# Sums of squares of keys and queries: put out by ScalarE's squares, one head at a time, in place of VectorE's sums

## The chip, the cores and the metric

The kernel runs on one core of a Trainium2 chip. The metric is the device time of one execution in microseconds (us), lower is better. The time before is 2769.91 us, the median of three runs (2766.08 to 2769.93).

Engine names as in the profile: PE is TensorE, DVE is VectorE, ACT is ScalarE, POOL is GpSimd, SP is SyncE. PE's weight loads are shown apart, as PEld.

## The reference, cut to what matters

A decoder layer on `x` (4, 256, 512) with a context `ctx` (4, 1601, 512), all fp32: a small attention over features, a cross attention of 32 query heads over 8 key/value heads, and a top-8 router, with a layer norm after each. The cross attention is nearly all of the work:

```
kv = concat([ctx, x])                       # 1857 rows per batch
q = (x @ Wq)  -> 32 heads of 128;  k, v = (kv @ Wk), (kv @ Wv) -> 8 heads of 128
q, k = rms_norm(q), rms_norm(k)             # per row and head: t * rsqrt(mean(t^2) + 1e-6) * w
probs = softmax(q k^T / sqrt(128));  out = (probs v) @ Wo
```

The change is about `mean(t^2)` in the two norms: for each row and head the 128 squares have to be summed.

## The kernel before, in words

One unit `v` is one batch and one key/value head: 4 x 8 = 32 units, some 80 us each. A unit has 15 tiles of key rows (the last has 65 rows) and two halves of 512 queries (2 heads x 256 rows), so 30 score tiles. All engines walk through the same list of steps `s`, one score tile for each step. In a step PE computes the score tile (`S_ps<-QT,KT`), does a piece of other work taken from `fill(s)` (projections of the next unit's keys and values into `K_ps`, of its queries, transposes of keys `KT` and queries `QT`, output products `O`), and multiplies a tile of probabilities that is 20 steps older with V (`OT_ps`). High precision comes from splitting an fp32 operand in a high and a low half and doing three products (lines 1015 to 1017); for some tiles (`FULL`) one plain fp32 product is used (L1045).

ACT in a step, in this order: `exp` of the tile 18 steps back (L1410 the rounded high half `P_hi` where the tile is split, L1411 the full one), the copy and scaling of the new score tile (`copy_scores`, L1397), high halves (`high`), the copies of new keys (`copy_keys`, L1505), `squares`, then the high half of a weight chunk (`split`, L1552). POOL: the low half of the probabilities (`lo`, L932, waits for ACT's L1411), their running sum (`add`, L950), the Newton steps of the rsqrt (`newton`, L959 to L974), low halves of weights (L989, wait for ACT's L1552). DVE: shift of a tile by its maximum (L1743), the running maximum (L1756, L1759, waits for ACT's L1397), the sums of squares, low halves, and what else is small. Each engine's queue is in order.

PE takes a new score tile into one of two banks, so it waits until DVE's running maximum has read the tile two before. It multiplies a split tile of probabilities with V only when POOL's `P_lo` is there.

**The norms.** Keys come in groups of four tiles (the last of three): four groups a unit, each with one `squares` on ACT when its keys are in `nat` (L1522, from SBUF), and the queries in two items a unit (L1526, from the PSUM bank). `sum_squares` on DVE reduces `sq` over each head's 128 columns (L1767, L1770); for queries it also copies the bank to `natq` (L1774) and frees it. So there are 128 + 64 = 192 items. Two steps later ACT's `rsqrt` (L1449, L1451) takes the sums, and POOL's `newton` after it.

Of the kernel before, what the change touches and what calls it, by code (L numbers as in the profile page):

```python
# [21 lines left out]
ACT = mybir.ActivationFunctionType  # L22
AX = mybir.AxisListType
# [22 lines left out]
def layer(nc, x_in, sWq, sbq, sWk, sbk, sWv, sbv, ctx_in, Wq, Wk, Wv, Wo, qw, kw, x1, y_out, Wr, rb, eb, final):  # L46
    B, L, E = ctx_in.shape
    S = x1.shape[1]
    HD = P
    KVH = Wk.shape[1] // HD  # L50
    GR = Wq.shape[1] // HD // KVH
# [38 lines left out]
    GROUPS = [list(range(4 * g, min(4 * g + 4, NJ))) for g in range(-(-NJ // 4))]  # L90
# [3 lines left out]
    def rows_of(j):  # L94
        return P if j < NJ - 1 else TAIL
# [39 lines left out]
    at = (UNITS - 7) * CYCLE - AHEAD  # L135
    ROUTE[at + 4].append(("load weights", 0))
    ROUTE_PE[at + 19].append(("FR",))
    for b in range(B - 1):
        at = (UNITS - 6 + 2 * b) * CYCLE - AHEAD
# [97 lines left out]
    for s in range(WAIT + 4, WAIT + NS):  # L237
        p, j = divmod(s - WAIT, NJ)
# [3 lines left out]
    for t in range(TPB, SELF):  # L242
        at = EVENTS[14 * (t - TPB):14 * (t - TPB) + 14]
# [23 lines left out]
    K_AT = {x: n for n, x in enumerate(K_ITEMS)}  # L267
# [13 lines left out]
    SQ_AT = {x: n for n, (_, x) in enumerate(SQUARED)}  # L281
# [43 lines left out]
    def left(kind, v, at):  # L325
        return NJ * (2 * v - 3) + max(kind[v - 2][at]) + 1 if kind[v - 2][at] else 0
# [8 lines left out]
    with ExitStack() as ctx:  # L335
        def sb(name, shape, dt=F32):
            return ctx.enter_context(nc.sbuf_tensor(name, shape, dt))

        def ps(name):
            return ctx.enter_context(nc.psum_tensor(name, [P, 512], F32))  # L340

        def sem(name):
            return ctx.enter_context(nc.semaphore(name))
# [26 lines left out]
        nat = [sb(f"nat{i}", [P, 4, HD]) for i in range(2)]  # L370
        natq = [sb(f"natq{i}", [P, GR, HD]) for i in range(TPB)]
        sq = sb("sq", [P, 4, HD])
# [65 lines left out]
        ss_k = sb("ss_k", [P, 2, 16])  # L438
        rk = sb("rk", [P, 2, 16])
        ss_q = sb("ss_q", [P, 8])  # L440
# [7 lines left out]
        K_ps = [ps(f"K_ps{i}") for i in range(2)]  # L448
# [121 lines left out]
        s_kr = sem("K_bank_free")  # L570
        s_kc = sem("K_rows_copied")
        s_vh = sem("V_hi_copied")
        s_sq = sem("squares")
        s_ss = sem("sum_of_squares")
        s_ln = sem("log_mean_square")
        s_y0 = sem("rsqrt_estimate")
# [32 lines left out]
        def pair_no(v, q):  # L609
            return 8 * v + q  # L610
# [706 lines left out]
        def _(e):  # L1317
# [175 lines left out]
            def copy_keys(v, q):  # L1493
                js = range(2 * q, min(2 * q + 2, NJ))
                r, k = rows_of(js[-1]), len(js)
                at = 2 * (q % 2)
                src = K_ps[K_AT["P", v, q] % 2][:].rearrange("p (k n) -> p k n", n=2 * HD)
                e.wait_ge(s_kt, 15 * v + js[-1] + 1)
                if q % 2 == 0:
                    g = q // 2  # L1500
                    if g >= 2 or v:

                        e.wait_ge(s_ff, F_AT["KT", v if g >= 2 else v - 1, (g - 2) % 4] + 1)
                        e.wait_ge(s_sq, SQ_AT["K", v if g >= 2 else v - 1, (g - 2) % 4] + 1)
                e.activation(nat[q // 2 % 2][0:r, at:at + k, :], src[0:r, 0:k, 0:HD], ACT.Copy).then_inc(s_kc, 1)  # L1505
                if (v, q) in HALF_PAIR_AT:
                    i = HALF[v].index(js[0])
                    if v >= 2:

                        e.wait_ge(s_pv, left(HALF, v, slice(i, i + k)))  # L1510
                    e.activation(V_hi[v % 2][0:r, i:i + k, :], src[0:r, 0:k, HD:2 * HD], ACT.Copy).then_inc(s_vh, 1)

            def squares(what):
                no = SQ_AT[what]
                if no:

                    e.wait_ge(s_ss, no)
                if what[0] == "K":
                    _, v, g = what
                    k = len(GROUPS[g])  # L1520
                    e.wait_ge(s_kc, pair_no(v, min(2 * g + 1, 7)) + 1)
                    e.activation(sq[:, 0:k, :], nat[g % 2][:, 0:k, :], ACT.Square).then_inc(s_sq, 1)  # L1522
                else:
                    _, v, t = what
                    e.wait_ge(s_qf, 2 * v + t + 1)
                    e.activation(sq[:].rearrange("p h d -> p (h d)"), K_ps[K_AT["Q", v, t] % 2][:], ACT.Square)\  # L1526
                        .then_inc(s_sq, 1)

            def split(chunk):
                n = W_AT[chunk]  # L1530
# [72 lines left out]
        def _(e):  # L1603
# [116 lines left out]
            def opening_self(part, t, i):  # L1720
                if part == "products":
                    self_products(t)
                elif part == "qk sum":
                    self_qk_sum(t, i)
                elif part == "max":
                    self_max(t)
                elif part == "normalise":
                    self_normalise(t)
                elif part == "pv sum":
                    self_pv_sum(t, i)  # L1730
                elif part == "residual":
                    self_residual(t)
                elif part == "layernorm":
                    self_layernorm(t)

            def shift(t):
                p, j = divmod(t, NJ)
                r = rows_of(j)
                if j == 0:
                    e.wait_ge(s_mb, p + 1)  # L1740
                e.wait_ge(s_cp, t + 1)
                d = row[t % RING][0:r, :]
                e.tensor_tensor(d, d, Mb_ps[0:r, :], ALU.add).then_inc(s_d, 1)  # L1743
# [14 lines left out]
                e.wait_ge(s_top, s)  # L1758
                e.scalar_tensor_tensor(a, src, k, a, ALU.mult, ALU.max).then_inc(s_top, 1)  # L1759

            def sum_squares(what):
                no = SQ_AT[what]
                e.wait_ge(s_sq, no + 1)
                if what[0] == "K":
                    _, v, g = what
                    k = len(GROUPS[g])
                    e.reduce_sum(ss_k[:, v % 2, 4 * g:4 * g + k], sq[:, 0:k, :], AX.X).then_inc(s_ss, 1)  # L1767
                else:
                    _, v, t = what
                    e.reduce_sum(ss_q[:, 4 * t:4 * t + 4], sq[:], AX.X).then_inc(s_ss, 1)  # L1770
                    if v:

                        e.wait_ge(s_ff, F_AT["QT", v - 1, 1] + 1)
                    e.tensor_copy(natq[t][:].rearrange("p h d -> p (h d)"), K_ps[K_AT["Q", v, t] % 2][:])\  # L1774
                        .then_inc(s_kr, 1)
# [151 lines left out]
            def block_max(p):  # L1927
                e.wait_ge(s_top, NJ * (p + 1))
                if p:

                    e.wait_ge(s_ff, F_AT["MT", p - 1] + 1)
                e.tensor_reduce(tops[:], top[:].rearrange("p (j a) -> p j a", a=32), AX.X, ALU.max, apply_transpose=True)\
                    .then_inc(s_bm, 1)
# [48 lines left out]
            for s in STEPS:  # L1982
                for part, t, i in SELF_AT[s]:
                    opening_self(part, t, i)
                if 0 <= s - WAIT < NS:
                    shift(s - WAIT)
                if 0 <= s - 1 < NS:
                    raise_max(s - 1)
                if 0 < s < NS and s % NJ == 0:
                    block_max(s // NJ - 1)  # L1990
                for what in squared(s - 1):
                    sum_squares(what)
                for x in fill(s - 1):
                    if x[0] not in ("KV", "Q", "MT") or x == ("MT", HALVES - 1):
                        drain(x)
                for v, q in pairs(s - 1):
                    low_values(v, q)
                for p in divided(s - 2):
                    OT_low(p)
                if s == NS:  # L2000
                    last_blocks()
                if s == NS + WAIT + LAG:
                    last_low()
                if 0 <= s - WAIT - 1 < NS and summed_tile(s - WAIT - 1):
                    sum_tile(s - WAIT - 1)
                for x in fill(s + 1):
                    if x[0] == "AT":
                        sum_blocks(x[1])
                for p in divided(s):
                    divide(p)  # L2010
                for part, t, i in LATER[s]:
                    later(part, t, i)
                for x in fill(s):
                    if x[0] == "MT" and x[1] not in LATE:
                        drain(x)
                for part, b in ROUTE[s]:
                    if part == "stats":
                        x2_stats(b, 2 * b)
                    elif part == "apply":
                        x2_apply(b, 2 * b)  # L2020
                    elif part == "shift":
                        router_shift(b)
                    elif part == "softmax":
                        router_softmax(b)
                    elif part == "top":
                        router_top(b)
                    elif part == "final stats":
                        x2_stats(b, 2 * b + 1)
                    elif part == "final apply":
                        x2_apply(b, 2 * b + 1)  # L2030
# [32 lines left out]
```

## Time and profile before

| | before |
|---|---|
| median of three runs | 2769.91 us |
| the profiled execution's own time | 2767.4 us |
| its span in the profile | 2765.6 us |
| mean granted TensorE clock | 0.993 |
| PE busy | 2694.3 us, 97% of the span |
| POOL busy | 2351.9 us, 85% |
| DVE busy | 2229.7 us, 81% |
| ACT busy | 2092.4 us, 76% |

A busy share is an average over the span; which engine sets the time at a place is read from what an instruction there waits for. In a timeline row the first number is the start in us from the span's start, the second the duration in us; a bracket at its end is the engine's idle time before it and who ended that. Neighbouring instructions of ACT overlap in these rows: the next one starts before the duration of the one before is over, so the distance of two starts is less than a duration. Line numbers (L...) are those of the kernel before.

### The profile page before, as it was taken

Reading aid. Unit: us, or ns where it says so; the run is one execution under the profiler, and the core shown is the slowest. Engines: PE = TensorE matmul, PEld = TensorE weight load, DVE = VectorE, ACT = ScalarE, POOL = GpSimd, SP = SyncE. Lnnn points to the kernel's source line nnn. Section 1 sums busy time; section 2 is a strip of 40 time slices with the busy share of each in tenths; the row PEclk is TensorE's granted clock in tenths of the full one; section 3 lists DMA queues with packets and bytes.
Section 4 is the critical chain, followed back from the end, with each engine's and each line's share of the span. In section 5 each row is a group of like instructions: output and inputs, shape, how many; then the busy total and the mean of one; then the engine's idle time right before and its main releaser. Section 6 shows DMA issues by size and latency. Waiting matters only on the chain.

```text
span 2765.6 us, 47104 instructions
## 1 busy us (share of the span) xinstructions
PE 2694.3 (97%) x14256; PEld 2146.5 (78%) x14256; DVE 2229.7 (81%) x3623; ACT 2092.4 (76%) x4202; POOL 2351.9 (85%) x2300
## 2 busy tenths in 40 slices
PE   7899999999999999999999999999999999999997
PEld 5777777777777788787788888888888887878864
DVE  5488888888888888888888777787777888888887
ACT  2578777787777777777788888788887777777774
POOL 4299999998889888888899888999899888889894
PEclk8999999999999999999999999999999999999999
DMA  6656655665655555555456555445544534444321
GB/s 218 249 198 205 222 194 187 214 209 172 212 176 170 183 180 179 176 188 166 173 173 203 175 184 190 159 171 171 195 158 170 184 130 165 153 164 168 115 66 53
DMA packets 160793, 485.33 MB, mean 175 GB/s; under 512 B 18583, under 2 KB 29337, under 8 KB 160542
## 3 DMA queue, kind: packets, MB, share of 16 engines
q1 hardware_dynamic: 158952, 480.75, 51.3%
q8 instruction: 116, 1.90, 0.3%
q10 hardware_dynamic: 1590, 1.58, 0.2%
q14 instruction: 135, 1.11, 0.1%
HBM read 402.83 MB, written 79.43 MB: 174 GB/s over the span
## 4 chain that ended last, share of the span: by engine, by line
PE 80%; POOL 7%; issue 6%; DVE 5%; ACT 2%; DMA 1%; SPq 0%; POOLq 0%; DVEq 0%; ACTq 0%
PE K_ps L1015 9%; PE K_ps L1017 9%; PE K_ps L1016 9%; PE S_ps L1015 7%; PE OT_ps L1045 7%; PE S_ps L1017 7%; PE S_ps L1016 7%; PE OT_ps L1015 5%; PE OT_ps L1016 5%; PE OT_ps L1017 5%; POOL acc L950 4%; POOL P_lo L932 2%; PE F_ps L1015 2%; PE F_ps L1016 2%; PE F_ps L1017 2%
## 5 line engine op out<-in xcount | busy, mean ns | idle before, releaser
L950 POOL TENSOR_TENSOR acc<-acc,scores 128x512 f32<-128x512 f32 x813 | 1080.5, 1329 | 53.8 <-ACT scores L1411 27.4
L932 POOL TENSOR_TENSOR P_lo<-scores,P_hi 128x512 fp32r<-128x512 f32 x672 | 913.1, 1360 | 186.5 <-ACT scores L1411 184.6
L1759 DVE SCALAR_TENSOR_TENSOR running_max<-S_ps,rk,running_max 128x512 f32<-128x512 f32 (+1 forms) x896 | 667.6, 745 | 274.9 <-ACT scores L1397 272.3
L1397 ACT ACTIVATE scores<-S_ps,rk 128x512 f32<-128x512 f32 (+1 forms) x960 | 650.7, 678 | 74.3 <-PE S_ps L1017 59.4
L1743 DVE TENSOR_TENSOR scores<-scores,Mb_ps 128x512 f32<-128x512 f32 (+1 forms) x960 | 644.5, 671 | 54.1 <-PE Mb_ps L1185 52.8
L1411 ACT ACTIVATE scores<-scores 128x512 f32<-128x512 f32 (+1 forms) x960 | 597.3, 622 | 96.0 <-DVE scores L1743 94.8
L1410 ACT ACTIVATE P_hi<-scores 128x512 fp32r<-128x512 f32 x672 | 423.4, 630 | 270.7 <-DVE scores L1743 193.7
L1015 PE MATMUL S_ps<-QT_hi,KT_hi 128*128 128x512 f32 (+1 forms) x960 | 495.5, 516 | 15.4 <-DVE running_max L1759 14.4
L1015 PE MATMUL K_ps<-Wkv_hi,kvT 128*128 128x256 f32 (+1 forms) x1664 | 470.5, 283 | 8.2 <-DVE kvT L1809 7.8
L1017 PE MATMUL K_ps<-Wkv_hi,kvT 128*128 128x256 f32 (+1 forms) x1664 | 469.6, 282 | 0.0
L1016 PE MATMUL K_ps<-Wkv_lo,kvT 128*128 128x256 f32 (+1 forms) x1664 | 468.7, 282 | 0.0
L1017 PE MATMUL S_ps<-QT_hi,KT_lo 128*128 128x512 f32 (+1 forms) x960 | 379.3, 395 | 0.0
L1016 PE MATMUL S_ps<-QT_lo,KT_hi 128*128 128x512 f32 (+1 forms) x960 | 378.0, 394 | 0.0
L1015 PEld LDWEIGHTS K_ps<-Wkv_hi,kvT 128*128 128x128 f32 (+1 forms) x1664 | 309.1, 186 | 31.4 <-DVE kvT L1809 8.7
L1016 PEld LDWEIGHTS K_ps<-Wkv_lo,kvT 128*128 128x128 f32 (+1 forms) x1664 | 309.2, 186 | 19.7
L1017 PEld LDWEIGHTS K_ps<-Wkv_hi,kvT 128*128 128x128 f32 (+1 forms) x1664 | 309.7, 186 | 0.0
L1015 PE MATMUL OT_ps<-P_hi,V_hi 128*128 128x512 f32 x672 | 286.5, 426 | 13.3 <-POOL P_lo L932 12.8
L1045 PE MATMUL OT_ps<-scores,V_full 128*128 128x512 f32 (+1 forms) x576 | 295.1, 594 | 0.0
L1015 PEld LDWEIGHTS S_ps<-QT_hi,KT_hi 128*128 128x128 f32 (+1 forms) x960 | 177.0, 184 | 139.4 <-issue 59.0
L1016 PE MATMUL OT_ps<-P_lo,V_hi 128*128 128x512 f32 x672 | 265.7, 395 | 0.0
L1017 PE MATMUL OT_ps<-P_hi,V_lo 128*128 128x512 f32 x672 | 265.1, 394 | 0.0
L1016 PEld LDWEIGHTS S_ps<-QT_lo,KT_hi 128*128 128x128 f32 (+1 forms) x960 | 177.9, 185 | 91.5 <-issue 63.0
(256 smaller groups left out, 4619.2 us busy)
## 6 DMA issues: line engine op xcount, KB each, us to landing
kvT<-kvT_scratch SPq DMA_DIRECT2D x403, 512.0 KB, 4.0
Wq_hi<-weight_halves_scratch SPq DMA_DIRECT2D x48, 512.0 KB, 5.8
Wq_lo<-weight_halves_scratch SPq DMA_DIRECT2D x48, 512.0 KB, 6.8
Wo_hi<-weight_halves_scratch SPq DMA_DIRECT2D x48, 512.0 KB, 4.6
Wo_lo<-weight_halves_scratch SPq DMA_DIRECT2D x48, 512.0 KB, 5.8
kvT_scratch<-built SPq DMA_DIRECT2D x45, 512.0 KB, 3.8
rinv_spread<-rinv_scratch SPq DMA_DIRECT2D x63, 256.0 KB, 5.3
Wkv_hi<-weight_halves_scratch SPq DMA_DIRECT2D x24, 512.0 KB, 5.5
```

The source lines that it names most:

```text
L932: e.tensor_tensor(P_lo[n % PB][0:r, :], prob(t)[0:r, :], f(P_hi[n % PB][0:r, :]), ALU.subtract)\
L950: e.tensor_tensor(a[0:r, :], a[0:r, :], prob(t)[0:r, :], ALU.add).then_inc(s_acc, 1)
L1015: e.matmul(out, l_hi, r_hi, start=first, stop=False)
L1016: e.matmul(out, l_hi, r_lo, start=False, stop=False)
L1017: return e.matmul(out, l_lo, r_hi, start=False, stop=last)
L1045: ins = e.matmul(OT_ps[:], V_full[v % 2][0:r, FULL[v].index(j), :], row[t % RING][0:r, :], start=first, stop=last)
L1397: e.activation(row[s % RING][0:r, :], S_ps[s % 2][0:r, :], ACT.Copy, scale=rk[0:r, v % 2, j:j + 1])\
L1410: e.activation(P_hi[n % PB][0:r, :], d, ACT.Exp)
L1411: e.activation(d, d, ACT.Exp).then_inc(s_p, 1)
L1743: e.tensor_tensor(d, d, Mb_ps[0:r, :], ALU.add).then_inc(s_d, 1)
L1759: e.scalar_tensor_tensor(a, src, k, a, ALU.mult, ALU.max).then_inc(s_top, 1)
```

## The change

ACT's square takes `accum_out`, which puts the sum along the free dimension in one column. One such instruction gives one sum for each row, so an item's one instruction over four heads becomes four over 128 columns each (three for the last key group). DVE's sums go; its copy of the queries stays and waits for the last of the four squares. The semaphore of the squares goes, and `s_ss` (the sums) is now counted up by ACT. ACT's wait for DVE's last sum before it overwrites `sq` goes too.

```
@@ copy_keys (ACT)
-                        e.wait_ge(s_sq, SQ_AT["K", v if g >= 2 else v - 1, (g - 2) % 4] + 1)
+                        e.wait_ge(s_ss, SQ_AT["K", v if g >= 2 else v - 1, (g - 2) % 4] + 1)
@@ squares (ACT)
-                if no:
-                    e.wait_ge(s_ss, no)
...
-                    e.activation(sq[:, 0:k, :], nat[g % 2][:, 0:k, :], ACT.Square).then_inc(s_sq, 1)
+                    for i in range(k):
+                        at = 4 * g + i
+                        ins = e.activation(sq[:, i, :], nat[g % 2][:, i, :], ACT.Square, accum_out=ss_k[:, v % 2, at:at + 1])
+                    ins.then_inc(s_ss, 1)
...
-                    e.activation(sq[:].rearrange("p h d -> p (h d)"), K_ps[K_AT["Q", v, t] % 2][:], ACT.Square)\
-                        .then_inc(s_sq, 1)
+                    for h in range(GR):
+                        at = 4 * t + h
+                        ins = e.activation(sq[:, h, :], K_ps[K_AT["Q", v, t] % 2][:, h * HD:(h + 1) * HD], ACT.Square,
+                                           accum_out=ss_q[:, at:at + 1])
+                    ins.then_inc(s_ss, 1)
@@ sum_squares -> copy_queries (DVE)
-                e.wait_ge(s_sq, no + 1)
-                    e.reduce_sum(ss_k[:, v % 2, 4 * g:4 * g + k], sq[:, 0:k, :], AX.X).then_inc(s_ss, 1)
-                    e.reduce_sum(ss_q[:, 4 * t:4 * t + 4], sq[:], AX.X).then_inc(s_ss, 1)
+            def copy_queries(what):
+                if what[0] == "Q":
                     _, v, t = what
+                    e.wait_ge(s_ss, SQ_AT[what] + 1)
```

## Rows read from the trace of the kernel before

**Rows 1.** The page's first part: span, and busy time of each engine.

```profile
span 2765.6 us, 47104 instructions
PE 2694.3 (97%) x14256; PEld 2146.5 (78%) x14256; DVE 2229.7 (81%) x3623; ACT 2092.4 (76%) x4202; POOL 2351.9 (85%) x2300
```

**Rows 2.** Windows: us, then busy us of PE, PEld, DVE, ACT, POOL; clock; DMA.

```profile
100.00:900.00 800.00, 781.76 (x4122) 614.84 (x4121) 658.76 (x1035) 611.68 (x1205) 705.27 (x670) 1.00 0.60 203
900.00:1480.00 580.00, 579.22 (x3104) 466.18 (x3103) 475.54 (x764) 451.11 (x915) 502.90 (x499) 1.00 0.53 179
```

**Rows 3.** Waits of PE from 100 to 2650 us: total us, times, longest.

```profile
PE S_ps L1015 <- DVE running_max L1759: 13.8, 15, 2.3
PE OT_ps L1015 <- POOL P_lo L932: 4.6, 6, 1.8
```

**Rows 4.** ACT's groups by form: count, busy us, mean ns of one, idle before.

```profile
L1522 ACT ACTIVATE sq<-nat 128x512 f32<-128x512 f32 x96 | 60.7, 632 | 4.9 <-ACT nat L1505 0.8
...
L1526 ACT ACTIVATE sq<-K_ps 128x512 f32<-128x512 f32 x64 | 38.2, 598 | 43.2 <-PE K_ps L1017 43.2
...
L1451 ACT ACTIVATE nrm_c<-nrm_c 128x3 f32<-128x3 f32 x32 | 6.5, 204 | 1.0
...
L1368 ACT ACTIVATE self_x<-self_x 128x128 f32<-128x128 f32 x4 | 1.2, 306 | 6.3 <-DVE self_x L1902 6.3
```

**Rows 5.** DVE's groups by form: the sums that go.

```profile
L1767 DVE TENSOR_REDUCE ss_k<-sq 128x4 f32<-128x512 f32 x96 | 64.9, 676 | 49.9 <-ACT sq L1522 49.9
...
L1770 DVE TENSOR_REDUCE ss_q<-sq 128x4 f32<-128x512 f32 x64 | 43.6, 682 | 20.4 <-ACT sq L1526 20.0
...
L1767 DVE TENSOR_REDUCE ss_k<-sq 128x3 f32<-128x384 f32 x32 | 17.6, 552 | 7.1 <-ACT sq L1522 5.6
```

**Rows 6.** Timeline of ACT around the second key group's square, one unit.

```profile
1391.57 1.27 ACT L1437 ACTIVATE natq<-natq,rq 128x128 f32<-128x128 f32 x4
...
1395.98 0.63 ACT L1522 ACTIVATE sq<-nat 128x512 f32<-128x512 f32 x1
1396.52 0.61 ACT L1410 ACTIVATE P_hi<-scores 128x512 fp32r<-128x512 f32 x1
1397.04 0.61 ACT L1411 ACTIVATE scores<-scores 128x512 f32<-128x512 f32 x1
```

**Rows 7.** Timeline of POOL after that square, in three units.

```profile
742.55 2.38 POOL L989 TENSOR_TENSOR Wo_lo<-w_stage,Wo_hi 128x1024 fp32r<-128x1024 f32 x1 [0.81 <-ACT Wo_hi L1552]
...
749.24 1.74 POOL L932 TENSOR_TENSOR P_lo<-scores,P_hi 128x512 fp32r<-128x512 f32 x1
...
1397.73 1.30 POOL L932 TENSOR_TENSOR P_lo<-scores,P_hi 128x512 fp32r<-128x512 f32 x1 [1.24 <-ACT scores L1411]
...
1400.22 1.77 POOL L932 TENSOR_TENSOR P_lo<-scores,P_hi 128x512 fp32r<-128x512 f32 x1
...
1404.62 1.75 POOL L932 TENSOR_TENSOR P_lo<-scores,P_hi 128x512 fp32r<-128x512 f32 x1
...
1646.94 1.75 POOL L932 TENSOR_TENSOR P_lo<-scores,P_hi 128x512 fp32r<-128x512 f32 x1
```

**Rows 8.** Timeline of PE: the products that take those low halves, five units.

```profile
245.65 0.50 PE L1015 MATMUL OT_ps<-P_hi,V_hi 128*128 128x512 f32 x1
...
751.03 0.50 PE L1015 MATMUL OT_ps<-P_hi,V_hi 128*128 128x512 f32 x1
...
916.41 0.50 PE L1015 MATMUL OT_ps<-P_hi,V_hi 128*128 128x512 f32 x1
...
1406.42 0.50 PE L1015 MATMUL OT_ps<-P_hi,V_hi 128*128 128x512 f32 x1
...
1649.38 0.48 PE L1015 MATMUL OT_ps<-P_hi,V_hi 128*128 128x512 f32 x1
```

**Rows 9.** Timeline of DVE after the second key group's square, one unit.

```profile
739.89 0.69 DVE L1767 TENSOR_REDUCE ss_k<-sq 128x4 f32<-128x512 f32 x1 [1.47 <-ACT sq L1522]
...
742.74 2.74 DVE L1963 TENSOR_TENSOR OT_n<-OT_n,rinv_spread 128x512 f32<-128x512 f32 x1
```

More of the change, by code:

```diff
@@ L572, in layer @@
         s_vh = sem("V_hi_copied")
-        s_sq = sem("squares")
         s_ss = sem("sum_of_squares")
@@ L1759, in raise_max @@
                 e.scalar_tensor_tensor(a, src, k, a, ALU.mult, ALU.max).then_inc(s_top, 1)
-            def sum_squares(what):
-                no = SQ_AT[what]
-                e.wait_ge(s_sq, no + 1)
-                if what[0] == "K":
-                    _, v, g = what
-                    k = len(GROUPS[g])
-                    e.reduce_sum(ss_k[:, v % 2, 4 * g:4 * g + k], sq[:, 0:k, :], AX.X).then_inc(s_ss, 1)
-                else:
+            def copy_queries(what):
+                if what[0] == "Q":
                     _, v, t = what
-                    e.reduce_sum(ss_q[:, 4 * t:4 * t + 4], sq[:], AX.X).then_inc(s_ss, 1)
+                    e.wait_ge(s_ss, SQ_AT[what] + 1)
                     if v:
@@ L1991, in _ @@
                 for what in squared(s - 1):
-                    sum_squares(what)
+                    copy_queries(what)
                 for x in fill(s - 1):
```

## The prediction

> **What bounds the kernel.** I read the page's busy times first. PE works for 97% of the span, the others for 76 to 85% [rows 1]. Then the windows: between 900 and 1480 us PE is busy for 579.22 of 580 us, between 100 and 900 us for 781.76 of 800 [rows 2]. So PE is the bound, and work taken off another engine can give back only PE's idle time, while a delay on another engine costs time wherever it reaches PE. Then PE's waits: from 100 to 2650 us it waited 13.8 us for DVE's running maximum and 4.6 us for POOL's low halves [rows 3]. That is the purse from which a gain would have to come. Then the timelines of ACT, POOL and PE, one unit after the other, behind each of the six squares items of a unit, to see how far each engine is ahead of PE there.
>
> **What the change removes.** DVE loses 64.9 + 17.6 + 43.6 = 126 us of sums [rows 5]. At the item that I find critical (below), the sum was not what DVE was short of: DVE had idled 1.47 us waiting for ACT's square before it started the sum [rows 9]. The queries' copy on DVE still stands behind the squares. ACT's wait for the last sum is worth nothing: the idle time in front of its squares was ended by its own copy or by PE, never by DVE [rows 4]. Off the critical path the 126 us are worth nothing either.
>
> **What it adds.** An item was one instruction over 512 columns. It lasted 632 ns from SBUF and 598 from PSUM [rows 4], and the next instruction started 0.54 us after it, so neighbours overlap by 0.09 us [rows 6]. Now an item is four instructions of 128 columns. No row shows an ACT instruction with an accumulator output, so I bound it. A square of 128 columns should last what the exponential of that size did, 306 ns [rows 4], so two starts would be 0.306 - 0.09 = 0.216 us apart.
> - Lower end, the sum costs nothing: 4 x 0.216 = 0.86 us, which is d = 0.86 - 0.54 = 0.32 us more for an item.
> - Upper end, each sum is written by a further step as long as ACT's smallest instruction, 204 ns [rows 4], with no overlap anywhere: 4 x (0.306 + 0.204) = 2.04 us, d = 1.50.
> - In between, that step exists and overlaps as all else does: 4 x (0.216 + 0.204 - 0.09) = 1.32 us, d = 0.78.
> I take 0.35 us a head, because a sum can only be put out once its square's last column is through and some overlap will be lost there: 1.40 us, d = 0.86. Five of a unit's six items have four heads and one has three, so ACT gains some 5 us a unit of 80 to 84 us, 32 x 5 = 160 us in all: from 76% to 81% busy [rows 1]. It does not become the bound. What counts is where an item's delay reaches PE.
>
> "ScalarE: Activation LUTs" of the Trainium skill, section "What ACT_TABLE_LOAD costs", has 186 ns + 0.833 ns a column for an ACTIVATE with immediate scale and bias and 93 ns of overlap, so 0.20 us from start to start for 128 columns, against my 0.216. It has no price for the accumulator. "VectorE: DVE Perf Modes", section "Two Vector instructions with no wait between them", says of its engine that an instruction which writes out its accumulator is two instructions; if ACT does it alike at the first page's fixed price (93 ns between starts), an item takes 1.17 us, d = 0.63, and the sum below would be 13 x 0.63 = 8.2 us and not 12.4: 2775.6 us. No row here can show it.
>
> **Where the delay lands.** Behind five of a unit's six items ACT soon has idle time, or POOL's low half comes well before PE wants it. One item is different: the second key group, whose square stands between query normalising (1391.57) and the exponentials (1396.52, 1397.04) in an ACT queue without a gap [rows 6].
> - Units between 900 and 1480 us: POOL waits 1.24 us for the exponential right behind this square and starts the low half at 1397.73; from there it runs without a pause (the low halves of 1400.22 and 1404.62 are in that run, with sums and Newton steps between), and the last ends at 1404.62 + 1.75 = 1406.37. PE's product with it starts at 1406.42, 0.05 us later [rows 7, 8], and lasts 0.50 us, which is long for that shape: it was waiting. Each later start on ACT passes through whole: d of PE's time. The same 0.05 us stands in seven units, first and last at 916.41 and 1406.42 [rows 8].
> - Units between 230 and 750 us: here POOL waits 0.81 us for ACT's weight copy, which comes behind the square in the same step, and starts at 742.55; again no pause, until the low half of 749.24 ends at 750.98 and PE starts at 751.03 [rows 7, 8]. Six units, first and last at 245.65 and 751.03 [rows 8]. Again d each.
> - Units between 1640 and 2130 us, seven: the low half ends at 1646.94 + 1.75 = 1648.69, PE starts at 1649.38: 0.69 us in hand [rows 7, 8], so d - 0.69 each.
> - Later units and the other items: nothing.
>
> Sum: 13 x 0.86 + 7 x 0.17 = 11.2 + 1.2 = 12.4 us. On the profiled execution (2767.4 us, span 2765.6) that gives 2779.8. The median of the three runs, 2769.9, is 2.5 us above that execution; on it the sum gives 2782.3. I say 2781. By the ends: d = 0.32 gives 4.2 us, 2771.6; d = 1.50 gives 13 x 1.50 + 7 x 0.81 = 25.2 us, 2792.6, or 2795 on the median. If the delays of neighbouring items then run together, a little more.
>
> **The rivals.**
> - *The sums are nearly free (no change), 18%.* d near 0.32 or below, the 4.2 us are lost in the spread of the runs, 2766.08 to 2769.93; 2772. For it: POOL and PE may settle in another order in which the lock of 0.05 us is gone. Against: four fixed costs for one.
> - *ACT pays the full price, 17%.* d = 1.50, 2793 to 2797; from d = 0.69 on, the units after 1640 us pay too. For it: no row says that the step overlaps.
> - *DVE's relief reaches PE (faster), 7%.* PE's 15 waits for the running maximum hold 13.8 us [rows 3]. If each shrank by one sum of 0.68 us [rows 5] that would be 10 us, 2758. It decides only if d is under some 0.1 us, since the running maximum itself stands behind ACT's copy of the scores, which stands behind the square. Against: DVE's 1.47 us of idle in front of the sum, and that the long piece of that stretch is a product of 2.74 us at 742.74, which stays [rows 9].
> - *The forecast, 58%.*
>
> A tie within 0.2% (5.5 us, about what a measurement can tell here) is what d up to some 0.4 us gives. Slower: the forecast nearly whole and the full price, 0.75. Same 0.18. Faster 0.07. The range of 2768 to 2797 leaves out the faster case and takes in both ends of d.
>
> **What would show each step.** ACT's rows for the squares: 736 instructions of some 0.3 us, perhaps as many small ones beside them, and from the first start of an item to the next foreign instruction 1.4 us. ACT busy near 2250 us, DVE near 2104. PE's waits for POOL's `P_lo` or a longer first product once a unit before 1480 us, some 0.9 us each; units there longer by 0.9 us, units after 2130 us as long as before. Wrong would be: an item of 0.9 us or of 2 us (the size of d), no wait at PE although ACT is later (slack that I took for a lock), or PE's waits for the running maximum that grow (a second path, through the copy of the scores).

## The result and the profile after

The changed kernel took 2776.98 us (median of 10 runs, 2774.72 to 2782.14), the kernel before 2768.96 us beside it (10 runs, 2764.93 to 2772.22). The ratio is 1.0037, 95% interval 1.0029 to 1.0045: 8 us slower by the medians, 8.0 to 12.5 by the interval. The forecast was 2781 us and slower; its sum was 12.4 us of delay. The profiled execution of the changed kernel is the fastest of its ten (2774.72 us); it has a span of 2772.9 us at a mean granted clock of 0.995.

First the page's busy times, to be read beside [rows 1].

```profile
span 2772.9 us, 48063 instructions
...
PE 2689.7 (97%) x14256; PEld 2143.2 (77%) x14256; DVE 2137.3 (77%) x3431; ACT 2185.2 (79%) x5482; POOL 2345.8 (85%) x2300
```

ACT gained 93 us, DVE lost 92, PE does the same 14256 matmuls. The windows (columns as in [rows 2]; the last two stretches were not shown before):

```profile
100.00:900.00 800.00, 780.20 (x4103) 613.76 (x4103) 617.23 (x976) 640.16 (x1596) 706.40 (x668) 1.00 0.60 203
900.00:1480.00 580.00, 577.35 (x3084) 462.32 (x3083) 455.37 (x720) 468.09 (x1191) 498.57 (x496) 1.00 0.52 178
1480.00:2130.00 650.00, 650.00 (x3551) 534.32 (x3550) 494.89 (x783) 549.87 (x1388) 580.62 (x586) 1.00 0.52 176
2130.00:2650.00 520.00, 508.00 (x2739) 411.64 (x2737) 423.02 (x692) 411.26 (x1046) 444.47 (x440) 1.00 0.44 148
```

The last of these before:

```profile
2130.00:2650.00 520.00, 514.96 (x2783) 417.01 (x2782) 440.05 (x742) 399.87 (x819) 449.60 (x444) 1.00 0.45 151
```

From 1480 to 2130 us PE has no idle time at all. From 2130 to 2650 us it idles 12.0 us; before, 5.0. PE's waits from 100 to 2650 us, to be read beside [rows 3]:

```profile
PE S_ps L1014 <- DVE running_max L1761: 14.7, 19, 2.0
PE OT_ps L1014 <- POOL P_lo L931: 11.8, 12, 1.8
PE Mb_ps L1184 <- DVE scores L1745: 4.3, 4, 1.5
```

The waits for POOL's low halves are twice as many, 12 for 6. Those for the running maximum hold much the same time, but 6.7 of the 14.7 us now stand behind 2130 us, where it was 1.9 of 13.8.

ACT's groups of the squares, by form; there are the 736 squares that the forecast named, and as many small instructions beside them:

```profile
L1520 ACT ACTIVATE sq<-nat 128x128 f32<-128x128 f32 x480 | 142.6, 303 | 2.5
L1520 ACT ACTIVATION_READ_ACCUMULATOR sq<-nat 128x1 f32 x480 | 92.1, 192 | 0.0
L1527 ACT ACTIVATE sq<-K_ps 128x128 f32<-128x128 f32 x256 | 67.3, 279 | 39.8 <-PE K_ps L1016 37.9
...
L1527 ACT ACTIVATION_READ_ACCUMULATOR sq<-K_ps 128x1 f32 x256 | 53.5, 209 | 0.0
```

And the timeline of ACT at the item of [rows 6]:

```profile
1392.90 0.31 ACT L1520 ACTIVATE sq<-nat 128x128 f32<-128x128 f32 x1
1393.12 0.18 ACT L1520 ACTIVATION_READ_ACCUMULATOR sq<-nat 128x1 f32 x1
1393.21 0.29 ACT L1520 ACTIVATE sq<-nat 128x128 f32<-128x128 f32 x1
...
1394.09 0.61 ACT L1409 ACTIVATE P_hi<-scores 128x512 fp32r<-128x512 f32 x1
1394.61 0.62 ACT L1410 ACTIVATE scores<-scores 128x512 f32<-128x512 f32 x1
```

Each sum is a second instruction of 0.18 us, but it overlaps with its neighbours: the next square starts 0.09 us after it. An item goes from 1392.90 to 1394.09 = 1.19 us where it took 0.54, so d is 0.65 us.

**Where the time went, unit by unit.** I took the distance between the first score tile's matmuls of neighbouring units in each trace and subtracted that of before; a unit lasts 76 to 85 us. In us, units added up as headed:

```
                       0-8    9-17   18-24  25-30
after                 +0.1    +4.3   +0.1   +8.4
units1to31_only       +0.8    +4.7   +0.1   +9.0
act_cost_alone        +5.8    +6.2   +0.4   +8.6
no_sums_no_split      -4.2    -1.3    0.0   +5.5
unit0_only            +2.0    +0.5    0.0   -0.3
group1_only           +2.6    +4.2   +0.1   +0.7
new_up_to_unit24      +2.2    +4.0   +0.1   -0.4
new_without_group1_to_unit24
                      -1.6    +0.3    0.0   -0.4
group1_two_steps_later
                      -2.2    +2.3    0.0   -0.3
split_no_accum        +4.3    +3.3    0.0   +0.4
router_one_source     +0.9    +3.8   +0.1   +2.6
```

The units' rows are of one execution each, and one thing in them doesn't follow the form of a unit: a stretch of some 2 to 3 us in which PE ran at the lower of its two clock levels (1.2 in place of 2.4 GHz). unit0_only shows what one costs. Its unit 2 has the form of before and the idle time of before, and is 1.57 us longer:

```profile
324.00:329.00 5.00, 4.67 (x20) 3.95 (x21) 4.46 (x9) 4.65 (x10) 4.44 (x9) 0.67 0.79 289
```

The granted clock there is 0.67, the third number from the end; in the execution of before it is 1.00 from 324 to 329 us. Such a stretch lies in the first column of unit0_only, split_no_accum, new_up_to_unit24 and group1_two_steps_later, and in the last column of after, units1to31_only, act_cost_alone, no_sums_no_split and router_one_source, once in each. Differences of 1.5 us between two rows of the table are not read below where one of them has it.

Ahead of unit 0 the changed kernel's execution is 7.2 us early (first score tile at 79.28 us, before at 86.43), and behind the last unit 1.3 us late. Much of both is the chance of the one execution of before: group1_only, whose unit 0 has the form of before, is 4.4 us early, and unit0_only, whose last units have it, is 2.3 us late. Of the 7.2 us the experiments below bear out some 2.5, of the 1.3 nothing.

### The profile page after: what moved, and what is told of

Read it like the earlier page. It is cut to its first block, busy times and chain, and to the rows that moved or that the text cites. A ratio compares the mean times of both kernels' runs of the same rounds, so it can differ in the third digit from the quotient of the medians.

```text
span 2772.9 us, 48063 instructions
## 1 busy us (share of the span) xinstructions
PE 2689.7 (97%) x14256; PEld 2143.2 (77%) x14256; DVE 2137.3 (77%) x3431; ACT 2185.2 (79%) x5482; POOL 2345.8 (85%) x2300
## 3 DMA queue, kind: packets, MB, share of 16 engines
q14 instruction: 143, 1.17, 0.1%
## 4 chain that ended last, share of the span: by engine, by line
PE 66%; POOL 16%; issue 10%; DVE 4%; ACT 2%; DMA 1%; SPq 0%; POOLq 0%; DVEq 0%; ACTq 0%
POOL acc L949 9%; PE K_ps L1014 7%; PE K_ps L1016 7%; PE K_ps L1015 7%; PE S_ps L1014 6%; PE OT_ps L1044 6%; PE S_ps L1016 5%; PE S_ps L1015 5%; PE OT_ps L1014 4%; POOL P_lo L931 4%; PE OT_ps L1015 4%; PE OT_ps L1016 4%; PE F_ps L1014 2%; PE F_ps L1016 2%; PE F_ps L1015 2%
```

## Experiments

Each ratio is to runs of the kernel before beside it. In the kernels that mix both forms, ACT's wait for the last sum ahead of a square stays; `by_act` says which items have the new form. Diffs are cut to the lines that matter.

**Opening or steady state.** One kernel has the new form in unit 0 alone, one in all the others.

```diff
+    def by_act(what):
+        kind, v, g = what
+        return v == 0          # second kernel: v > 0
```

> New form (four squares with sums on ACT) in unit 0 alone, whose items lie in the opening, before the steady part; units 1 to 31 as before. Theory A (the opening's gain is real and belongs to the change: with DVE's sum out of the chain PE waits less at 46 us and its clock stays up, 0.96 against 0.80 granted between 40 and 90 us): the first score tile starts some 5 to 7 us earlier than before, at about 79 to 81 us, and the whole kernel is 4 to 7 us faster than before. Rival B (the 7.2 us were a lucky opening of that one execution): no difference that can be measured, first score tile anywhere between 79 and 87 us.

> The complement: unit 0 as before, new form in units 1 to 31. Theory A: the loss of the steady part (15 us in the changed kernel's trace) without the opening's gain, so 12 to 15 us slower than before. Rival B: the same as the changed kernel, some 8 us slower than before. If the steady part's losses hang on how engines happen to stand to each other and not on the items (rival C), it can be anything from 0 to 15.

Measured: unit0_only 2766.12 us (12 runs), ratio 0.9995 (0.9987 to 1.0003); units1to31_only 2783.5 us (6 runs), ratio 1.0058 (1.0045 to 1.0071). So the loss is in units 1 to 31, and the opening gives back less than the 4 to 7 us I had expected: 1.4 us by unit0_only, which its interval doesn't part from nothing. The two ratios of 1.0037 and 1.0058 would put it at 5.8 us, 1.6 to 10 by their intervals, so some 2 to 3.5 us agree with both. What a trace of it holds is this, in PE's waits of before, from 40 to 80 us:

```profile
46.52 0.58 PE L1015 MATMUL K_ps<-Wkv_hi,kvT 128*128 128x256 f32 x1 [3.17 <-DVE kvT L1809]
...
77.99 0.39 PE L1015 MATMUL K_ps<-Wkv_hi,kvT 128*128 128x256 f32 x1 [3.31 <-DVE kvT L1809]
```

and after:

```profile
44.24 0.39 PE L1014 MATMUL K_ps<-Wkv_hi,kvT 128*128 128x256 f32 x1 [2.55 <-DVE kvT L1805]
...
70.79 0.39 PE L1014 MATMUL K_ps<-Wkv_hi,kvT 128*128 128x256 f32 x1 [1.41 <-DVE kvT L1805]
```

DVE has one sum less before the chunk that PE waits for. The pair reads 2.53 and 1.41 in unit0_only and 2.58 and 1.41 in no_sums_no_split, but 3.13 and 3.31 in units1to31_only, which keeps the sums there: 0.6 + 1.9 = 2.5 us, in every trace with the new unit 0. The rest of the 7.2 us is the chance of one execution. The granted clock between 40 and 80 us was 0.78 in the trace of before and 0.96 in that of after, but 0.85 to 0.91 in units1to31_only, act_cost_alone, no_sums_no_split and unit0_only, in no order that follows the change.

**Each half of the change alone.** One kernel drops DVE's sums and leaves ACT's single square; nobody sums the squares then, the sums are constants, and keys and queries are not normalised. The other pays ACT's price and keeps DVE's sums.

```diff
-                    e.reduce_sum(ss_k[:, v % 2, 4 * g:4 * g + k], sq[:, 0:k, :], AX.X).then_inc(s_ss, 1)
...
-                    e.reduce_sum(ss_q[:, 4 * t:4 * t + 4], sq[:], AX.X).then_inc(s_ss, 1)
...
+            e.memset(ss_k[:], 128.0).then_inc(s_pad, 1)
+            e.memset(ss_q[:], 128.0).then_inc(s_pad, 1)
```

> DVE's relief alone: the squares on ACT are one instruction as before and nobody sums them; the sums are constants of 128, so keys and queries are not normalised (the output is not the reference's). ACT's load as before, DVE's 126 us of sums gone. Theory A: the opening's gain is there (4 to 7 us), the waits at PE for the running maximum in units 2 to 8 shrink, nothing is lost in units 9 to 15: 5 to 9 us faster than before. For units 26 to 31: if their loss of 1.9 us each comes from DVE's earlier small operations falling on POOL's (theory D), it shows here too, and the kernel is only 0 to 4 us faster; if it comes from ACT's later instructions (rival E), it does not show.

```diff
-                    e.activation(sq[:, 0:k, :], nat[g % 2][:, 0:k, :], ACT.Square).then_inc(s_sq, 1)
+                    for i in range(k):
+                        ins = e.activation(sq[:, i, :], nat[g % 2][:, i, :], ACT.Square, accum_out=spare[:, i:i + 1])
+                    ins.then_inc(s_sq, 1)
```

> ACT's cost alone: an item is four squares with sums as in the change, but the sums go to a spare tile that nobody reads, and DVE still makes its own sums. d = 0.65 us on ACT for an item as in the change, no relief on DVE. Theory A with my locks: the opening is not faster, units 2 to 8 and 9 to 15 lose 0.5 to 0.65 us each, 13 x 0.6 = 8 us, and with the opening's longer chain 8 to 12 us slower than before. Theory D for units 26 to 31: no loss of 1.9 us there; rival E: the loss is there, 15 to 20 us slower in all.

Measured: no_sums_no_split 2759.25 us (7 runs), 0.9975 (0.9963 to 0.9987); act_cost_alone 2791.84 us (4 runs), 1.0088 (1.0075 to 1.0102). The relief is worth some 7 us and the price some 24, more than the 8 to 12 or 15 to 20 that I had expected: every unit from 0 to 17 but one is half a us longer or more, also those that the forecast gave no lock. In units 1 to 7 the two halves are -4.4 and +4.5 us, and after has -0.2: there they add up. Behind unit 24 they don't: +5.5 and +8.6, and after has +8.4, so removing DVE's work makes even the cheap version lose there. One theory had the loss for the relief alone, its rival for ACT's price alone; that each brings it was in neither, and led to the next experiments.

**Which item, which units.**

```diff
-        return v == 0                                                  # of unit0_only
+        return kind == "K" and g == 1 and v > 0                        # group1_only
+        return v < 25                                                  # new_up_to_unit24
+        return v == 0 or (v < 25 and not (kind == "K" and g == 1))     # new_without_group1_to_unit24
```

> New form only for the second key group of units 1 to 31, all else as before. Theory A (one item of six, the one behind which POOL runs without a pause into PE's product, makes the whole loss up to unit 17): units 9 to 15 get 0.6 us longer as with the full change, units 4 to 8 0.3 to 0.6 us; 8 to 10 us in units 1 to 17. Units 26, 28 and 30, where the loss begins behind the first key group's square, stay as before: 8 to 10 us slower than before in all. Rival F (the loss is spread over all items): 1 to 3 us slower, one item's share.

> New form in units 0 to 24, as before from unit 25. Theory A: the opening's 2.5 us, the units up to 17 as in the changed kernel, and units 26 to 30 as long as before, since what is lost there hangs on the items there: 8 to 9 us faster than the changed kernel, 0 to 3 us slower than before. Rival G (units 26 to 30 lose because the whole schedule has come to stand differently by then): their 1.9 us stay, and it is as slow as the changed kernel.

> What the findings so far would pick: new form in unit 0 and in units 1 to 24 for every item but the second key group, as before from unit 25. Theory A: DVE's relief stays (the opening's 2.5 us of PE's waits, about 1 us in each of units 1 to 3), ACT's delay falls where it has slack: 3 to 7 us faster than before. Rival F: the other five items' delays reach PE too, the units are as long as in the changed kernel, and it is 0 to 4 us slower than before.

Measured: group1_only 2773.45 us (11 runs), 1.0019 (1.001 to 1.0028); new_up_to_unit24 2769.87 us (11 runs), 1.0005 (0.9996 to 1.0014); new_without_group1_to_unit24 2763.76 us (11 runs), 0.9987 (0.9978 to 0.9996). One item of a unit's six brings the whole loss of the middle units (+4.2 of +4.3 us in units 9 to 17), and leaving it out takes that loss away (+0.3). As a whole group1_only loses 2.8 to 7.7 us by its interval, where I had expected 8 to 10. The new form from unit 25 on costs (1.0037 - 1.0005) x 2769 = 9 us, as the table has it (8.4 + 0.4).

**Does the accumulator set the price?** The four squares without `accum_out`, DVE's sums kept:

```diff
-                        ins = e.activation(sq[:, i, :], nat[g % 2][:, i, :], ACT.Square, accum_out=spare[:, i:i + 1])
+                        ins = e.activation(sq[:, i, :], nat[g % 2][:, i, :], ACT.Square)
```

> ACT's squares split over the heads (four of 128 columns) but without sums; DVE makes its own sums as before. This is the lower end of the price: from start to start 0.2 us a head, d = 4 x 0.20 - 0.54 = 0.26 us an item in place of 0.65. Theory A (d goes through whole at the second key group): units 4 to 15 get some 0.25 us longer each, 12 to 16 units, 3 to 4 us; units 26, 28 and 30 lose 1 to 2 us each if the product of the router has already left its gap beside POOL's operation, 0 if it has not: 3 to 10 us slower than before, and nothing gained. Rival (some slack swallows a small d): units 4 to 15 as before.

Measured: 2774.86 us (7 runs), 1.0026 (1.0014 to 1.0037). Its ACT timeline at the same item:

```profile
1397.42 0.91 ACT L1523 ACTIVATE sq<-nat 128x128 f32<-128x128 f32 x4
1398.24 0.61 ACT L1410 ACTIVATE P_hi<-scores 128x512 fp32r<-128x512 f32 x1
```

Four squares from 1397.42 to 1398.24 = 0.82 us, d = 0.28 without an accumulator, and its units 8 to 15 are mostly 0.3 us longer, where act_cost_alone's are 0.65 longer: PE loses d at both sizes of d. That is the lock that the forecast read from 0.05 us.

**Is it the item's place?** As new_up_to_unit24, with that item's squares issued two steps later, right ahead of the `rsqrt` that takes the sums.

```diff
+                for what in squared(s - 2):
+                    if put_off(what):          # kind == "K" and g == 1 and 0 < v < 25
+                        squares(what)
                 for kind, v in rooted(s - 2):
                     rsqrt(kind, v)
```

> New form in units 0 to 24 for all items, as before from unit 25 (as in new_up_to_unit24), and in units 1 to 24 the second key group's squares are issued two steps later on ACT, just ahead of the rsqrt that takes their sums, so that the exponential which POOL waits for is not behind them. Theory A: the 0.6 us a unit of units 9 to 15 are gone although ACT does the same work: 4 to 7 us faster than new_up_to_unit24, 2 to 5 us faster than before. Rival (ACT's added work reaches PE wherever it stands): the same as new_up_to_unit24.

Measured: 2763.53 us (11 runs), 0.9985 (0.9976 to 0.9994), 5.5 us less than with the item in its old place by the ratios: where the item stands is what costs. The move isn't free everywhere: its units 10 and 14 are still 1.07 and 0.91 us longer than before, and why is open. This and the version without the item are the fastest here that compute the reference's output, 4 us under the kernel before.

**The late units.** In the kernel after, the router's product and subtraction on DVE are replaced by a form with one source, a copy; the division of the softmax and the subtraction are left out, so its output is not the reference's.

```diff
-                e.tensor_tensor(f_ex, f_ex, f_soft[:, 2, :].unsqueeze(2).to_broadcast([P, TPB, NE]), ALU.mult)\
-                    .then_inc(sf_pr, 1)
+                e.reduce_sum(f_ex, f_ex.unsqueeze(3), AX.X).then_inc(sf_pr, 1)
...
-                e.tensor_tensor(f_rest, f_ex, f_rest, ALU.subtract).then_inc(sf_tk, 1)
+                e.reduce_sum(f_rest, f_rest.unsqueeze(3), AX.X).then_inc(sf_tk, 1)
```

> The changed kernel with two of the router's DVE operations, each with two SBUF operands (the softmax's product by its reciprocals and the subtraction of what is left after the top 8), replaced by a reduction over a last axis of one element, which reads one operand and copies it in place. The division and the subtraction are left out, so the output is not the reference's. Theory D (these two last 1.38 and 1.05 us in units 26, 28, 30 in place of 0.42 and 0.29 because they share a port with a POOL operation in flight): both last 0.25 to 0.4 us, PE's wait for the running maximum there falls from 2.0 us to under 0.7 us, units 26, 28 and 30 are 1.2 to 1.9 us shorter each than in the changed kernel: 4 to 6 us faster than it, 2 to 5 us slower than before. Rival E (ACT's delay itself reaches PE there): no shorter than the changed kernel.

Measured: 2770.45 us (11 runs), 1.001 (1.0001 to 1.0019). Units 26, 28 and 30, which after are 1.87, 1.84 and 1.88 us longer than before, are -0.05, -0.05 and -0.07 here. The rows, first DVE's timeline of after:

```profile
2228.39 1.38 DVE L1907 TENSOR_TENSOR self_x<-self_x,self_small 128x128 f32<-128x128 f32 x1
...
2234.52 1.05 DVE L1919 TENSOR_TENSOR self_x<-self_x 128x128 f32<-128x128 f32 x1
```

POOL's beside it, and the wait of PE that comes of it:

```profile
2228.35 1.28 POOL L945 TENSOR_TENSOR acc<-scores 128x512 f32<-128x512 f32 x1
```

```profile
2238.04 0.50 PE L1014 MATMUL S_ps<-QT_hi,KT_hi 128*128 128x512 f32 x1 [2.04 <-DVE running_max L1761]
```

The same three places before, where POOL starts after DVE:

```profile
2230.78 0.42 DVE L1911 TENSOR_TENSOR self_x<-self_x,self_small 128x128 f32<-128x128 f32 x1
...
2231.01 1.34 POOL L946 TENSOR_TENSOR acc<-scores 128x512 f32<-128x512 f32 x1
...
2238.92 0.51 PE L1015 MATMUL S_ps<-QT_hi,KT_hi 128*128 128x512 f32 x1 [0.62 <-DVE running_max L1759]
```

And with one source, beside POOL's sum in flight:

```profile
2231.94 1.28 POOL L945 TENSOR_TENSOR acc<-scores 128x512 f32<-128x512 f32 x1
2231.98 0.29 DVE L1907 TENSOR_REDUCE self_x<-self_x 128x128 f32<-128x128 f32 x1
```

```profile
2239.71 0.50 PE L1014 MATMUL S_ps<-QT_hi,KT_hi 128*128 128x512 f32 x1 [0.58 <-DVE running_max L1761]
```

DVE's product starts 0.04 us after POOL's sum and lasts until it is over (2228.35 + 1.28 = 2229.63, DVE's next starts at 2229.70); before, it starts 0.23 us ahead of POOL's and lasts 0.42. With one source it isn't held, and PE's wait is 0.58 us in place of 2.04. "SBUF — State Buffer" of the Trainium skill, section "Who interferes with whom", has this rule: a DVE instruction with two SBUF inputs contends with a GpSimd instruction that reads SBUF, a reduction doesn't, and whoever issues first goes first. The trace agrees: 0.42 us ahead, 1.38 behind, 0.29 as a reduction.

## Why the prediction was right, and where not

**The bound and the purse: right.** PE was the bound before and is after. "The 126 us are worth nothing" was nearly right: their removal alone gave 7 us (no_sums_no_split). DVE's busy time fell by 102 us there and not by 126, because neighbours overlap, and by 92 between before and after: the forecast's 2104 us for DVE was 33 too low.

**The price of an item: right in kind, too high in size.** I took 0.35 us a head and d = 0.86; rows of the critical item show 0.30 a head and d = 0.65. The step of 204 ns is there (192 from SBUF, 209 from PSUM), and the loss of overlap that I added is not; without it my 0.33 was still 0.03 too high. The rows are in keeping with the estimate that stood beside the sum (1.17 us, d = 0.63), which was made from "VectorE: DVE Perf Modes" of the Trainium skill, section "Two Vector instructions with no wait between them": an accumulator output is a second instruction there, and here on ACT too. ACT's busy time rose by 93 us and not by 160, to 2185 and not 2250; 192 items at 0.65 would be 125 us, and the three-head items (0.89 us) and those from PSUM (1.01) are cheaper.

**Seven units from 900 to 1480 us, d each: right.** With the true d the term is 7 x 0.65 = 4.55 us. The units that start with unit 9 are longer by 1.17, 0.78, 0.64, 0.14, 0.66, 0.61 and 0.56 = 4.56. That the two sums are equal is chance: unit 9 has 0.65 in router_one_source, and unit 12, at 0.14, has 0.63 in group1_only; the other five show d. POOL's last low half and PE's product after it, first POOL's timeline:

```profile
1395.30 1.29 POOL L931 TENSOR_TENSOR P_lo<-scores,P_hi 128x512 fp32r<-128x512 f32 x1 [1.83 <-ACT scores L1410]
...
1402.17 1.75 POOL L931 TENSOR_TENSOR P_lo<-scores,P_hi 128x512 fp32r<-128x512 f32 x1
```

```profile
1403.97 0.50 PE L1014 MATMUL OT_ps<-P_hi,V_hi 128*128 128x512 f32 x1
```

POOL still has no pause there, ends at 1402.17 + 1.75 = 1403.92, and PE starts 0.05 us later, as in [rows 7, 8]. The forecast left one such unit out, between its two stretches. In unit 8, before,

```profile
835.00 0.50 PE L1015 MATMUL OT_ps<-P_hi,V_hi 128*128 128x512 f32 x1 [1.77 <-POOL P_lo L932]
```

starts 0.05 us behind POOL too, and the unit is 0.65 us longer after.

**Six units from 230 to 750 us, d each: half right.** ACT's price is paid there (act_cost_alone: 0.55 to 0.74 in each of units 1 to 7), but DVE's relief, which I had priced at nothing, gives it back. The piece that I said "stays", 2.74 us at 742.74 [rows 9], did not. After, DVE's timeline has

```profile
734.86 0.68 DVE L1959 TENSOR_TENSOR OT_n<-OT_n,rinv_spread 128x512 f32<-128x512 f32 x1
```

and POOL's and PE's

```profile
735.10 2.68 POOL L988 TENSOR_TENSOR Wo_lo<-w_stage,Wo_hi 128x1024 fp32r<-128x1024 f32 x1 [0.80 <-ACT Wo_hi L1554]
...
742.05 1.27 POOL L931 TENSOR_TENSOR P_lo<-scores,P_hi 128x512 fp32r<-128x512 f32 x1
```

```profile
737.92 0.50 PE L1014 MATMUL S_ps<-QT_hi,KT_hi 128*128 128x512 f32 x1 [0.17 <-DVE running_max L1761]
...
743.38 0.50 PE L1014 MATMUL OT_ps<-P_hi,V_hi 128*128 128x512 f32 x1 [1.24 <-POOL P_lo L931]
```

DVE's product now starts 0.24 us ahead of POOL's weight half and takes 0.68 us; before, it started 0.19 behind it [rows 7, 9] and took 2.74. PE waits 0.17 us for the running maximum behind that place, where it waited 0.95, and pays 1.24 at the low half. It is so in all of units 1 to 7: the product takes 1.5 to 2.8 us before and 0.68 after. It takes 0.68 too in group1_only, where the second key group's sum is the only one of the unit that DVE lost, and as long as before in new_without_group1_to_unit24, which keeps that sum and drops the unit's others, and in split_no_accum. So it is this sum, five instructions ahead of the product, whose going flips the two (with the item two steps later the units are mixed, 0.68 to 2.87). How much of the time given back is the flip's stays open: in units 1 to 7 act_cost_alone is 4.5 us longer than before, group1_only 2.1 and after -0.2.

**Seven units from 1640 to 2130 us, d - 0.69: right.** With d = 0.65 nothing is left, and units 18 to 24 are +0.1 together. But d doesn't arrive there whole. Of the 0.69 us in hand (1.23 in unit 24) act_cost_alone leaves 0.05 to 0.06 (0.60), that is, it takes d; after, where DVE has lost its sums, 0.53 (1.10) are left. The term came out right with room to spare.

**"Later units and the other items: nothing": this is the step that failed, for the later units.** For the other items it held where it could be read: in units 9 to 17 group1_only has all of the loss. Units 26 to 30 lose 1.87, 2.09, 1.84, 0.85 and 1.88 us, 8.5 in all, and not because an item is late at PE there: DVE's product with two sources falls behind POOL's sum in place of ahead of it. It does so when DVE is earlier (no_sums_no_split, product 1.38 us at 2219.46 beside POOL's at 2219.43), and units 26, 28 and 30 lose 2 us and more also where ACT is later (act_cost_alone), but not with d = 0.28 (split_no_accum) or with the second key group's item alone (group1_only). I had said the two halves' effects there would be nothing, and looked for waits only, not for neighbours that hold each other up. For units 26, 28 and 30 this is shown by router_one_source. Units 27 and 29 are another place of the same kind, not tested alone: `maxima_on_diagonal` on DVE, a product of two sources. Before and after, in unit 27:

```profile
2345.21 0.75 DVE L1833 TENSOR_TENSOR maxima_on_diagonal<-negated_maxima,ident 16x512 fp32r<-16x512 f32 x1
```

```profile
2344.48 1.49 DVE L1829 TENSOR_TENSOR maxima_on_diagonal<-negated_maxima,ident 16x512 fp32r<-16x512 f32 x1
```

After, it starts 0.36 us behind a POOL instruction of 1.29 us; before, 1.08 us behind one of 1.28. PE's wait behind it, first before, then after, in both units:

```profile
2349.12 0.46 PE L1185 MATMUL Mb_ps<-maxima_on_diagonal,one 16*128 16x512 f32 x1 [0.79 <-DVE scores L1743]
...
2516.64 0.46 PE L1185 MATMUL Mb_ps<-maxima_on_diagonal,one 16*128 16x512 f32 x1 [0.82 <-DVE scores L1743]
```

```profile
2349.11 0.46 PE L1184 MATMUL Mb_ps<-maxima_on_diagonal,one 16*128 16x512 f32 x1 [1.50 <-DVE scores L1745]
...
2350.67 0.42 PE L1014 MATMUL K_ps<-Wkv_hi,kvT 128*128 128x256 f32 x1
2350.88 0.42 PE L1015 MATMUL K_ps<-Wkv_lo,kvT 128*128 128x256 f32 x1
...
2520.83 0.46 PE L1184 MATMUL Mb_ps<-maxima_on_diagonal,one 16*128 16x512 f32 x1 [1.50 <-DVE scores L1745]
```

That is 0.7 us a unit, most of unit 29's 0.85. What unit 27 has beyond it is the clock. Its matmuls behind the wait start 0.21 us apart, elsewhere 0.12, until 2353.23, so they ran at the lower of the two levels (1.2 in place of 2.4 GHz); the granted clock from 2340 to 2356 us is 0.89, before 1.00. Behind the same wait in unit 29 it stays 1.00. Units 27 (+2.09) and 29 (+0.82) stay in router_one_source, which leaves this product as it is.

**The opening** was not in the sum. It gives 2.5 us by the traces.

**So the sum** for the whole, by the unit lengths, is 0.1 + 4.3 + 0.1 + 8.4 + 0.2 (unit 31) - 2.5 = 10.6 us, where the ratio says 8.0 to 12.5 by its interval. The forecast's 12.4 us came out near that partly by luck: 8.4 us in a place priced at nothing, more than 1 of them from the clock, stand for a price of an item that was a third too high and six units whose loss was given back.

**The rivals.** The sums are nearly free: refuted by d = 0.65. The full price: refuted by the overlap. DVE's relief reaches PE: it does, for 7 us when nothing is paid for it, though I had said that it could only with d under some 0.1 us, and the item of the second key group and the late units outweigh it; where these two are left alone (new_without_group1_to_unit24), the change is 4 us faster than before.

## What to carry to other kernels

Price a moved piece of work by the one place in a unit where its new engine has no gap before the bound engine, and try it without that item or with it a step later: five of six items were free here up to unit 24, one cost the gain. Before a difference of 1 or 2 us between two traces is read, compare the granted clock at that place. Where two engines share a path to memory, a shift of 0.2 us decides which of two neighbours is held, so look in the trace for long DVE instructions with two sources right behind or ahead of a POOL instruction, and count each within reach of the shift as a term of either sign.

## What was not expected of the hardware

- ACT's accumulator output is an instruction of its own, 192 ns (from SBUF) or 209 ns (from PSUM), but costs only 0.09 us from start to start: 0.30 us for square and sum of 128 columns from SBUF, against 0.20 without (split_no_accum), and 0.25 against 0.16 from PSUM.
- A DVE product of 128x128 with two sources from SBUF went from 0.42 to 1.38 us, a subtraction from 0.29 to 1.05, and one of 128x512 from 0.68 to 2.74, by starting 0.04 to 0.4 us behind a POOL instruction in place of just ahead of it.
- PE's wait of 1.50 us at 2349.11, where before it was 0.79, was followed by 3 us of matmuls 0.21 us apart in place of 0.12. The same wait at 2520.83 was not. A stretch at the lower level cost a unit 1.57 us in unit0_only, where nothing else had changed.
